# First cross attention: the side computation's sums on GpSimd, its division in two halves on VectorE

## The reference, cut to what matters

```python
x = _layernorm(x + _L0_xattn_ref(x, ctx, ctx, Wq, Wk, Wv))   # layer 0
```

```python
A2 = ew * A + ekt * vt          # scans over tokens, forward and backward
B2 = ew * Bd + ekt
cur = jnp.exp(uc + k)
wkv = (Af + Ab + cur * v) / (Bf + Bb + cur)
```

## Time and profile before

| | |
|---|---|
| three runs | 2579.5, 2586.76, 2589.91 us, median 2586.76 |
| the profiled execution's own time | 2564.78 us |
| its span, first to last instruction | 2562.7 us |
| mean granted TensorE clock | 0.913 of full speed |
| busy: PE, DVE, ACT, POOL | 2064.0 (81%), 1461.8 (57%), 937.0 (37%), 765.8 us (30%) |
| the stage of the change | from 216 to 372.5 us of the span |

### The profile page before, as it was taken

How to read it: one execution, slowest core, us unless ns; L and a number is a source line. 1 busy time by engine, 2 the same in 40 slices (tenths; PEclk the granted TensorE clock), 3 DMA queues, 4 the chain that set the end, 5 groups by cost and what they waited for, 6 DMA issues and landing times. The chain is left out here.

```text
span 2562.7 us, 36952 instructions
## 1 busy us (share of the span) xinstructions
PE 2064.0 (81%) x13951; PEld 1454.8 (57%) x13951; DVE 1461.8 (57%) x2966; ACT 937.0 (37%) x1539; POOL 765.8 (30%) x549
## 2 busy tenths in 40 slices
PE   7987748884895784699667876997999999777998
PEld 5765535552795673699345643683344444326787
DVE  3785874457233567111754634235799899993533
ACT  3333413321111352232434420113675756442443
POOL 1121321224002201100340104004688898972000
PEclk9999978996898886799889988998999999998999
DMA  4217010001895100797100012392210101001000
GB/s 158 75 42 251 14 52 16 1 18 55 324 382 202 48 19 17 300 365 270 56 25 2 2 60 74 90 267 78 74 46 21 49 18 54 13 1 54 1 17 17
DMA packets 104576, 232.64 MB, mean 91 GB/s; under 512 B 10000, under 2 KB 77456, under 8 KB 95568
## 3 DMA queue, kind: packets, MB, share of 16 engines
q1 hardware_dynamic: 95664, 208.24, 23.4%
q0 software_dynamic: 7680, 20.98, 2.5%
q10 hardware_dynamic: 1056, 1.05, 0.1%
HBM read 174.27 MB, written 55.97 MB: 90 GB/s over the span
## 5 line engine op out<-in xcount | busy, mean ns | idle before, releaser
L3638 POOL TENSOR_TENSOR l_attn_ring<-l_attn_ring,l_attn_c_rows 128x1024 f32<-128x1024 f32 x128 | 301.5, 2356 | 83.9 <-DVE l_attn_ring L3527 83.9
L3527 DVE TENSOR_TENSOR_SCAN l_attn_ring<-bank,l_attn_ring 128x512 f32<-128x512 f32 x256 | 299.1, 1210 | 23.2 <-ACT bank L3410 18.7
L3254 PE MATMUL bank<-l_attn_ring,identity 128*128 128x512 f32 x512 | 250.3, 612 | 36.2 <-POOL l_attn_ring L3638 29.3
L3410 ACT ACTIVATE bank<-l_attn_step,l_attn_minus_exp_a_log 128x508 f32<-128x508 f32 x256 | 173.6, 685 | 165.0 <-DVE l_attn_ring L3527 164.6
L164 PE MATMUL bank<-x_features,weights 128*128 128x512 f32 x416 | 206.0, 634 | 28.3 <-issue 15.1
L3254 PEld LDWEIGHTS bank<-l_attn_ring,identity 128*128 128x128 f32 x512 | 95.5, 194 | 150.4 <-issue 103.9
L470 DVE TENSOR_REDUCE negmax_slots<-bank 128x16 f32<-128x2048 f32 x48 | 109.8, 2287 | 97.5 <-PE bank L361 97.1
L3521 DVE TENSOR_TENSOR l_attn_ring<-l_attn_step_times_input,bank 128x1024 f32<-128x1024 f32 x128 | 153.2, 1197 | 1.9 <-issue 1.3
L164 PEld LDWEIGHTS bank<-x_features,weights 128*128 128x128 f32 x416 | 81.3, 202 | 124.5 <-issue 106.8
L3984 DVE TENSOR_TENSOR l_ffn_hidden_low<-weights,l_ffn_hidden_high 128x512 fp32r<-128x512 f32 x64 | 44.2, 692 | 98.5 <-ACT l_ffn_hidden_high L3967 98.5
L173 PE MATMUL bank<-weights,x_features 128*128 128x256 f32 (+1 forms) x320 | 96.0, 457 | 5.3 <-ACT x_features L2579 2.1
(11 more groups left out here) (676 smaller groups left out, 4477.1 us busy)
## 6 DMA issues: line engine op xcount, KB each, us to landing
l_attn_tile_weights<-l_ffn_experts SPq DMA_DIRECT2D x22, 2180.0 KB, 9.6
ffn_experts_tile_weights<-l_ffn_experts_experts SPq DMA_DIRECT2D x37, 1024.0 KB, 7.8
expert_slots<-zeros SPq DMA_DIRECT2D x8, 2048.0 KB, 11.5
l_attn_c_rows<-state_outputs SPq DMA_DIRECT2D x64, 256.0 KB, 3.2
l_ffn_tile_weights<-l_ffn_experts SPq DMA_DIRECT2D x23, 512.0 KB, 4.6
expert_slots<-residual_sum SPq DMA_DIRECT2D x62, 128.0 KB, 8.5
expert_slots<-zeros SPq DMA_DIRECT2D x1, 5888.0 KB, 28.7
l_ffn_tile_x<-expert_slots SPq DMA_DIRECT2D x23, 256.0 KB, 4.2
```

Source lines behind the costliest of these rows:

```text
L3254: mm = pe.matmul(net.banks[SUMS[j]][:], net.ident[:], ring[n % 4][:, j, :], start=s == 0, stop=s == STATES - 1)
L3410: nc.scalar.activation(by_seq(net.banks[DECAY[j]][:])[:, :, 1:], by_seq(dt[:, m, :])[:, :, 1:], ACT.Exp, scale=a[:, m * STATES + s:m * STA ...
L3527: nc.vector.tensor_tensor_scan(ring[n % 4][:, j, :], net.banks[DECAY[j]][:], ring[n % 4][:, j, :], 0.0, ALU.mult, ALU.add).then_inc(state_ ...
L3638: tt(ring[n % 4][:], ring[n % 4][:], c_row[:, n % STATES, :].unsqueeze(1).broadcast_to([P, 2, T]), ALU.mult).then_inc(out_ready, 1)
```

## The change

In the first cross attention alone (the first attention passes no `sums` and keeps its way), piece 2's four VectorE operations are replaced by six on GpSimd: for the denominator and then for the numerator a multiplication of exp(k) or exp(k) v with the bonus (tensor_scalar, in place), the addition of the two scans, and the addition of both, which waits for the two before it. They stand in pass 4n+1 of GpSimd's loop, ahead of the add of that pass, and wait for the four scans of the unit. A marker on GpSimd behind them now gives `used`. VectorE's pieces 2 and 3 become `divide_half`: piece 2 waits for the denominator and takes the reciprocal of two of the four sequences; piece 3 takes that of the other two, waits for the numerator and for the earlier stores, and multiplies all four.

```diff
--- before.py
+++ after.py
@@ -572,9 +572,10 @@
         self.scans = sb("scans", [P, 4, NB, PAD])
         self.out = sb("quotient", [P, T])
 
-    def begin(self, signals, first, end):
+    def begin(self, signals, first, end, sums=()):
 
         self.consts_ready, self.zeros_ready, self.ek_ready, self.ekv_ready, self.scanned, self.used, self.out_ready = signals
+        self.sums_ready = sums
         self.units = range(first, end)
         self.each = len(self.units) * self.PIECES // SEQUENCES
 
@@ -654,6 +655,8 @@
         elif i == 1:
             self.scan(n, self.ekv, 2, True)
             self.scan(n, self.ek, 3, True)
+        elif self.sums_ready:
+            self.divide_half(dve, chain, n, i - 2)
         elif i == 2:
             dve.wait_ge(self.scanned, 4 * (at + 1))
             for k, own in enumerate((self.ekv, self.ek)):
@@ -672,6 +675,35 @@
                 dve.wait_ge(self.net.wkv_stored, 16 * n)
             num, den = self.scans[:, 0, :, 0:P], self.scans[:, 1, :, 0:P]
             chain(nc.vector.reciprocal(den, den))
+            nc.vector.tensor_tensor(self.by_seq(self.out[:]), num, den, ALU.mult).then_inc(self.out_ready, 1)
+            dve.wait_ge(self.out_ready, at + 1)
+
+    def sums_pool(self, pool, step):
+
+        nc, (at, i) = self.net.nc, divmod(step, self.PIECES)
+        if i != 1 or at >= len(self.units):
+            return
+        f = self.units[at] % FT
+        pool.wait_ge(self.scanned, 4 * (at + 1))
+        for k, own in ((1, self.ek), (0, self.ekv)):
+            total, bonus, done = self.scans[:, k, :, 0:P], own[:, :, 1:P + 1], self.sums_ready[k]
+            nc.gpsimd.tensor_scalar(bonus, bonus, self.bonus[:, f:f + 1], None, ALU.mult).then_inc(done, 1)
+            nc.gpsimd.tensor_tensor(total, total, self.scans[:, 2 + k, :, 2:P + 2], ALU.add).then_inc(done, 1)
+            pool.wait_ge(done, 3 * at + 2)
+            nc.gpsimd.tensor_tensor(total, total, bonus, ALU.add).then_inc(done, 1)
+        pool.wait_ge(self.sums_ready[0], 3 * (at + 1))
+        nc.gpsimd.engine_nop().then_inc(self.used, 1)
+
+    def divide_half(self, dve, chain, n, half):
+        nc, at = self.net.nc, n - self.units[0]
+        of = slice(2 * half, 2 * half + 2)
+        num, den = self.scans[:, 0, :, 0:P], self.scans[:, 1, :, 0:P]
+        dve.wait_ge(self.sums_ready[1], 3 * (at + 1))
+        chain(nc.vector.reciprocal(den[:, of, :], den[:, of, :]))
+        if half:
+            dve.wait_ge(self.sums_ready[0], 3 * (at + 1))
+            if n:
+                dve.wait_ge(self.net.wkv_stored, 16 * n)
             nc.vector.tensor_tensor(self.by_seq(self.out[:]), num, den, ALU.mult).then_inc(self.out_ready, 1)
             dve.wait_ge(self.out_ready, at + 1)
 
@@ -1006,7 +1038,7 @@
     w = net.weights("l0_xattn")
     wq, wk, wv = (tiles(w[n], FT) for n in ("wq", "wk", "wv"))
     with ExitStack() as sub:
-        sig = net.signals(25)
+        sig = net.signals(27)
         added, rstd_ready, x_ready, dve_steps = sig[14:18]
 
         class Heads(Heads16):
@@ -1018,7 +1050,7 @@
                       lambda name: name[0] in "kq")
         norms = Norms(net, net.scratch(sub), "x", rstd_ready)
         wkv = net.wkv_sums
-        wkv.begin(sig[18:], FIRST_UNITS, wkv.UNITS)
+        wkv.begin(sig[18:25], FIRST_UNITS, wkv.UNITS, sig[25:])
         last = NB * (GROUPS - 1)
 
         with nc.Block() as block:
@@ -1097,6 +1129,7 @@
                 heads.run_pool()
                 for n in range(SEQUENCES):
                     wkv.product_pool(pool, n)
+                    wkv.sums_pool(pool, n)
                     pool.wait_ge(heads.context_ready, n + 1)
                     x = net.x_all[:, n, :]
                     nc.gpsimd.tensor_tensor(x, x, heads.context[:, n % NB, :], ALU.add).then_inc(added, 1)
```

## The result

The changed kernel took 2591.57 us (median of 12 runs, 2585.61 to 2595.95), the kernel before 2584.46 beside it (12 runs, 2577.53 to 2589.91). The ratio is 1.0027, interval 1.0016 to 1.0039: +7.1 us, with 4 to 10 allowed. The forecast was +12.0.

The account below looks back on a forecast made before the run. Bound by two chains, through VectorE or PE and ScalarE, in the first cross attention's sixteen steps; VectorE ends steps 5, 9, 13. Root stalls 13.2 + PE 1.0 - gains 2.2 = +12.0 on 2586.76: 2598.8 us, range 2584 to 2611.

Parts of the forecast that it names:

- the place and the mechanism: Steps 5, 9, 13: GpSimd's sums start with the layer norm's root and stall its VectorE instructions; PE already waits there.
- rival 2: Roots of steps 5, 9, 13: no stall worth the name, 2.2 us gained, 2584.6 us; chance 0.17.
- rival 3: Half reciprocal in step 2: the denominator comes late at VectorE, about +0.5 us, 2599.3 us in all; chance 0.05.
- the term of 4.4 us per root, 13.2 in all: Steps 5, 9, 13: layer norm's root, twelve tiny VectorE instructions, ends 7.5 us after the scans, not 3.1.
- the walk: Root's twelve instructions followed beside GpSimd's six after the scans: one passes per tensor_tensor, partial stall against tensor_scalar.
- The first rival: Roots: full stall behind tensor_scalar too, at 2.84 us each; 8.2 us late per root, +23.4, 2610.2 us; chance 0.17.
- Tensor_scalar at 1.21 us: GpSimd's sums: length taken for each 512-column single-operation tensor_scalar, half of 2.42, between 0.53 and 2.84.
- PE's term of 1.0: Steps 6 and 10: PE slower after its longer wait, 0.45 us each, 1.0 in all with the matmuls behind.
- The gains of 2.2: Step 11 gains 1.5 us from the halved reciprocal, step 14 gains 0.7 us from the sums leaving VectorE.
- the floor that I set at PE's scores: Step 14: scores that the row maximum reads are written until 354.61, which becomes late next; gain only 0.7 us.
- The last division, forecast at 0: After step 15 VectorE waits 1.95 us for PE, so the last division counts for nothing.

Follow-up runs that it names:

- additions back to back: Kernel before plus four idle GpSimd additions beside each root, each into its own place, without waits between (last one 400 columns): ratio 1.0052.
- tensor_scalar alone: Kernel before plus four idle GpSimd tensor_scalar multiplications, begun at the end of the scans of steps 5, 9 and 13: ratio 1.0025.
- the fills: Kernel before plus four GpSimd fills of 128x512, begun at the end of the scans of steps 5, 9 and 13: 2588.18 against 2582.07 us.
- the longer root: Kernel before plus 17 more tiny VectorE instructions behind each of the three roots, GpSimd idle: ratio 1.0038.
- the additions: Kernel before plus four GpSimd additions into an unused tile beside each root, each waiting for the one before: ratio 1.0033.

## Why the prediction was right and wrong

**Right: the place and the mechanism.** Steps 5, 9 and 13 lose, since GpSimd's sums start at the end of the scans, where the root starts, and PE already waits there. That the openings, a late start or enough small gaps would spare the root (rival 2) is excluded by the root at 6.16. Where a wait moved the sums behind the root, they cost it nothing, and steps 11 and 14 gave that rival's gain (2.15 together, 2.2 forecast). Steps 2, 3 and 7 did not change, as said; step 6, named with them, became 0.17 longer. No division waits for the denominator (rival 3): the half reciprocals follow the instruction before them at once.

**Wrong: the term of 4.4 us per root, 13.2 in all.** It measured 3.36, 10.1 in all. The step of the walk that failed is "one and a half of its instructions pass before 1.3, one each ends at 2.5 and 3.7, five pass by 4.9 at about 0.25 each, one each ends at 6.0 and 7.2, and two remain". The first tensor_scalar takes 1.56 and not 1.21, and two instructions pass in it before L249, the third, is held to its end. One slips through before the second addition, which the walk did not have. In the second tensor_scalar five pass, as said, but four of them at 0.16. So the root has its last instruction at the third addition and is over 6.5 us after the scans' end (270.74); the fourth addition holds nothing of it. The addition's own rate, one instruction held to its end, was right; the count of instructions that come to the dear stretches was not. The experiment with additions back to back shows that the openings alone don't decide this: the length saved and the instruction let through cancel there.

**The first rival** priced a full hold by tensor_scalar. The experiment with tensor_scalar alone excludes it (root +1.03 under four of them); for the additions the hold is full. The Trainium skill, "SBUF — State Buffer", section on SBUF's two sides, has the shared port pair locked for the whole instruction: the addition rows agree (1.00, 0.94, 1.11), the tensor_scalar rows do not (held 0.34 and 0.46 beyond the free 0.17 and 0.16, out of 1.56). The same section of the Trainium skill has VectorE's instructions with two SBUF inputs contend only with a GpSimd instruction that reads SBUF. No run here shows that second half, since the fills were over before the first of the nine began.

**Tensor_scalar at 1.21 us** measured 1.56, between the bounds 0.53 and 2.84, and nearer to the row that was chosen. The Trainium skill, "GPSIMD Engine Reference", section on elementwise cycle accounting, gives 769 ns for a tight loop over 512 elements. This trace does not agree for the tensor_scalar, which took twice that.

**PE's term of 1.0** measured 1.7: of the 11.29 us in steps 5, 9 and 13, the roots are 10.11 and the rest 1.18, and steps 6 and 10 add 0.51. Of it, 0.46 each in steps 5 and 9 is L407, as forecast. The rest is PE as well, at the lower granted clock. In step 13 the transposes of the context took 1.06 at a granted clock of 0.50 instead of 0.60 at 1.00, and VectorE, which waits for them, comes to its division 0.25 later in the step (0.85 us after the shift's start, not 0.60). The run with the longer root does not have this; why the clock stood lower there is open.

```profile
346.81 1.06 PE L416 MATMUL bank<-identity,l_xattn_context_slots 128*128 128x128 f32 x4
```

In steps 6 and 10 the first half of the scores took 2.09 in after, the row at 281.50 and its like, and 1.95 and 1.73 in before:

```profile
276.48 1.95 PE L361 MATMUL bank<-l_xattn_q_slots,l_xattn_k_slots 32*128 32x128 f32 x32 [0.34 <-DVE l_xattn_q_slots L480]
```

From the shift to the context matmuls it was 4.83 us in both steps, against 4.67 and 4.45. The experiment with the longer root, GpSimd idle, has the same 10.21 in steps 6 and 10, so this needs no work on GpSimd.

**The gains of 2.2** measured 3.35. Step 11 gave 1.63 for 1.5. Step 14 gave 1.72 for 0.7, because the floor that I set at PE's scores was not there: in before the second half of them took 1.93 at a granted clock of 0.50 (1.2 GHz), in after 1.06 at 1.00 (363.76), so that they end at 364.82 and the row maximum, at 365.02, starts behind VectorE's own work. That floor was a measured duration of one clock level, and I took it over as if it were fixed. The 1.0 us beyond the forecast came with the clock and was not foreseen.

**The last division, forecast at 0**, was worth 0 itself. Step 15 is 0.85 shorter because its context matmuls, behind the same wait of 2.00, took 1.08 at a granted clock of 1.00 and not 1.94 at 0.50:

```profile
362.32 1.94 PE L397 MATMUL bank<-l_xattn_probs,l_xattn_values_and_one 128*32 128x128 f32 x32 [2.00 <-ACT l_xattn_probs L451]
```

Two of the experiments, the additions and the longer root, have before's VectorE pieces and the same last step of 7.14, so it is not the division's doing. Between the kernels that ran, this step took from 6.68 to 8.07; what makes the chip grant one level or the other there, the runs don't show.

Together, against +12.0 forecast for the stage: roots -3.1, PE +0.7, gains -1.15, the end -0.85, which makes the +7.6 of the stage; the 7.1 measured agrees.

## What to carry to other kernels

Before work is moved to GpSimd, look at what VectorE does at the moment at which that work becomes ready: a chain of tiny dependent instructions is the worst company for it, since each one can be held for the length of a whole GpSimd addition, six times its own. Making GpSimd wait a few microseconds for that chain costs one wait, and turned +7.1 into -5.3 here. Moving the residual adds out of the scans' way as well took another 1.9 us off four steps of the profiled stage.

## What had not been expected of the hardware

- GpSimd's addition of 128x512 holds a tiny VectorE instruction to its end (0.89 to 1.11 instead of 0.16), but its tensor_scalar of 1.56 us only for 0.3 to 0.5 us near its start or end. Which end depends on VectorE's kind in these rows: L251, with two tensors, was free 0.70 us after the tensor_scalar's start (275.29 against 274.59); L249, with one, waited to its end (272.43 against 272.40).
- A fill holds VectorE's tensor_scalar to its end (0.42 to 0.55 instead of 0.17); whether it holds an instruction with two tensors, no run shows.
- A scan of 520 columns that began while GpSimd's residual add ran took 1.70, and 1.22 without the add; a scan that began before the add kept 1.23.
- PE's four transposes took 0.66 after a wait of 2.34 us and 1.11 after one of 5.71, at granted clocks of 1.00 and 0.50; the same matmuls of scores or context took 1.06 to 1.08 at a granted clock of 1.00 and 1.93 to 1.94 at 0.50.
